# Rotary casts on ScalarE, quarter steps on VectorE and a new slot table in a two-layer pipeline

## The reference

```python
# block 1, per row: 16 heads of 16
xn = rms(x) * g1;  Q, K, V = xn @ Wq.T, xn @ Wk.T, xn @ Wv.T;  Q, K = elu(Q), elu(K)
kv1 = sum_h K[:, h, :8]^T V[:, h] * s     # two 8x16 matrices per row
kv2 = sum_h K[:, h, 8:]^T V[:, h] * s
attn = Q1 kv1 - lmb * Q2 kv2              # per head, then rms per head * g2, rms per row * g3 + itself
out = gelu(attn @ W1.T) @ W2.T + attn
# block 2: 16 segments of 512 rows
q, k, v = rms(h) @ Wq, @ Wk, @ Wv         # 16 query heads, 4 key heads, rotary embedding on q and k
ctx = causal_softmax(q k^T / 4) v;  h = clip(h + ctx @ Wo)
w = top 2 of 8 of softmax(rms(h) @ Wr);  out = clip(h + sum_e w_e * (silu(h Wg_e) * (h Wu_e)) Wd_e)
```

## Time and profile before

| what | value |
|---|---|
| median of 3 runs | 4241.21 us |
| the profiled execution | 4237.51 us, span 4235.6 us |
| PE, DVE, ACT, POOL busy | 3146.7, 2483.6, 1599.7, 1651.6 us |
| granted PE clock, mean | 0.843 of 2.4 GHz |
| attention_kernel | to about 3250 us |
| experts_kernel and finish | from about 3250 us to the end |

### The profile page before, as it was taken

The page is one execution under the profiler, slowest core; times in us unless marked ns, Lnnn a source line. Parts: engine busy times, 40 slices in busy tenths (PEclk is TensorE's granted clock), DMA queues, the critical chain, the costliest instruction groups (busy, mean ns, idle before and its releaser), DMA issues. The chain is left out here.

```text
span 4235.6 us, 54665 instructions
## 1 busy us (share of the span) xinstructions
PE 3146.7 (74%) x17668; PEld 1857.1 (44%) x17669; DVE 2483.6 (59%) x5036; ACT 1599.7 (38%) x3644; POOL 1651.6 (39%) x2045
## 2 busy tenths in 40 slices
PE   3555777777767776777777677767887399999991
PEld 2433434443443444444434444443433266666660
DVE  4667776776677667767776776676563122222225
ACT  1222445444534443443345444435544122222223
POOL 4564433543553354345435443541312122222222
PEclk7677888788888888887888888888888699999995
DMA  1000000000000000000000000000000533333335
GB/s 36 3 9 7 7 9 9 10 19 7 22 14 14 14 15 21 9 19 9 20 7 20 16 13 13 14 17 6 21 16 30 161 61 55 55 60 56 55 52 164
DMA packets 102336, 123.25 MB, mean 29 GB/s; under 512 B 14048, under 2 KB 89824, under 8 KB 102112
## 3 DMA queue, kind: packets, MB, share of 16 engines
q1 hardware_dynamic: 76384, 85.54, 6.7%
q0 software_dynamic: 25728, 34.88, 4.8%
HBM read 58.23 MB, written 61.36 MB: 28 GB/s over the span
## 5 line engine op out<-in xcount | busy, mean ns | idle before, releaser
L752 ACT ACTIVATE PR<-SP_ 128x512 f32<-128x512 f32 (+3 forms) x1536 | 728.0, 490 | 1528.6 <-PE SP_ L1366 1019.0
L1042 DVE TENSOR_REDUCE NM<-MX 128x1 f32<-128x512 f32 (+3 forms) x1536 | 817.1, 551 | 657.3 <-PE MX L1322 398.2
L1319 PE MATMUL MX<-KST,QST 96*128 96x512 bf16 (+3 forms) x1536 | 540.6, 362 | 407.3 <-DVE NM L1042 353.9
L472 POOL TENSOR_TENSOR P<-QK,VS 128x2048 f32<-128x2048 f32 x128 | 478.8, 3740 | 860.8 <-DVE QK L863 860.8
L1363 PE MATMUL SP_<-QST,KST 99*128 99x512 bf16 (+3 forms) x1536 | 544.0, 357 | 67.4 <-ACT PR L752 53.7
L1319 PEld LDWEIGHTS MX<-KST,QST 96*128 96x128 bf16 x1536 | 155.8, 102 | 770.5 <-DVE NM L1042 560.4
L1646 POOL DMA_INDIRECT scratch_h<-Y,XG x136 | 211.6, 1556 | 632.4 <-DVE Y L1709 538.8
L1214 PE MATMUL SUM<-ident,P 128*128 128x128 f32 x2048 | 313.0, 319 | 138.1 <-POOL P L472 83.5
L1687 DVE TENSOR_TENSOR AG<-UB,SL 128x512 f32<-128x512 f32 x136 | 94.0, 691 | 488.5 <-PE UB L1726 488.5
L1380 PE MATMUL OA<-PR,V 128*32 128x512 f32 (+3 forms) x3072 | 354.4, 536 | 0.8 <-ACT PR L752 0.6
L1214 PEld LDWEIGHTS SUM<-ident,P 128*128 128x128 f32 x2048 | 285.3, 168 | 158.3 <-issue 68.8
(11 more groups left out here) (245 smaller groups left out, 5399.1 us busy)
## 6 DMA issues: line engine op xcount, KB each, us to landing
XG<-scratch_xs SPq DMA_DIRECT2D x136, 130.0 KB, 2.1
X<-in_L_attn_x SPq DMA_DIRECT2D x64, 128.0 KB
scratch_x<-X SPq DMA_DIRECT2D x64, 128.0 KB, 1.8
scratch_h<-H SPq DMA_DIRECT2D x64, 128.0 KB, 1.7
X<-scratch_x SPq DMA_DIRECT2D x16, 512.0 KB, 4.0
HH<-scratch_h SPq DMA_DIRECT2D x16, 512.0 KB
out<-X SPq DMA_DIRECT2D x16, 512.0 KB, 3.2
wg<-in_L_ffn_Wg SPq DMA_DIRECT2D x1, 4096.0 KB, 13.9
```

The costliest lines, as they stand in the source:

```text
L472: sg["prod1"].by(pool.tensor_tensor(P1[:, half].rearrange("p (h e d) -> p h e d", h=hh, e=HD), QK[:, t % 2, D:2 * D][:, r].rearrange("p (h ...
L752: sg["exp"].by(act.activation(PR[:, n % 8, q0:512], SP_[:, n % 2, q0:512], ACT.Exp))
L1042: sg["mx"].by(dve.tensor_reduce(NM[:, u % 2, part, i, h:h + 1], MX[:, index % 2, 0:n], AX.X, ALU.max, negate=True))
L1319: m = pe.matmul(out, QST[0:MROW, j % 2, g * G + h, i * P:(i + 1) * P], KST[0:MROW, keys % RK, g, 0:n], start=True, stop=not last)
```

## The change

1. **Casts to ACT.** DVE's `parts` is taken apart. DVE keeps the add and two subtractions (`add_rotated`, `first_rest`, `third_part`); the two casts and the copy become ACT steps `first_part`, `second_part`, `second_again`. Each hand-over is a semaphore wait. They stand in slots DVE 7, ACT 8, DVE 9, ACT 10, DVE 11 and ACT 11; POOL's `copies` goes from slot 4 to 12.
2. **Quarter steps.** P2 has two buffers of half the size; the products and sums come in eight instructions of 128x1024 (slots 16 to 23, 0 and 1).
3. **Logits ahead.** PE's `second_layer` goes to slot 3, ahead of `route` (slot 5); DVE's `logits` stands in slot 7. Logits are thus copied a full period before the next second layer.
4. **New slots.** Most other steps move by a few slots.

```diff
-        P2 = sb("P2", [P, H * D // 2])
+        P2 = sb("P2", [P, 2, H * D // 4])
@@ POOL
-                        if i == 2 and have(p):
+                        if i == 4 and have(p):
                             key_products(p, 0)
-                        if i == 4 and have(p - 8):
-                            copies(p - 8)
-                        if i == 6 and have(p):
+                        if i == 7 and have(p):
                             key_products(p, 1)
-                        if i == 8 and have(p - 1):
+                        if i == 9 and have(p - 1):
                             head_roots(p - 1)
                         if i == 10 and have(p - 6):
                             out_coefficients(p - 6)
+                        if i == 12 and have(p - 8):
+                            copies(p - 8)
@@ ACT
+                def first_part(t):
+                    need("turned", t + 1)
+                    if t >= 1:
+                        need("tpq", 2 * t)
+                        need("copies", 3 * t)
+                    sg["part1a"].by(act.activation(parts_of_all(0), whole, ACT.Copy))
+
+                def second_part(t):
+                    need("rest", t + 1)
+                    sg["part1b"].by(act.activation(parts_of_all(1), rest, ACT.Copy))
+
+                def second_again(t):
+                    need("part1b", t + 1)
+                    sg["part2q"].by(act.activation(q_stack[:, :, 5], q_stack[:, :, 1], ACT.Copy))
...
+                        if i == 8 and have(p - 8):
+                            first_part(p - 8)
+                        if i == 10 and have(p - 8):
+                            second_part(p - 8)
+                        if i == 11 and have(p - 8):
+                            second_again(p - 8)
+                        if i == 11 and have(p - 6):
+                            layer_normed(p - 6)
                         if i == 12 and have(p - 7):
                             projected(p - 7)
-                        if i == 13 and have(p - 6):
-                            layer_normed(p - 6)
+                        if i == 14 and have(p):
+                            sums_out(p)
@@ DVE
-                def query_products(t, half):
+                def query_products(t, k):
                     need("kv", t + 1)
-                    need("attn", 2 * t + half)
+                    need("attn", 4 * t + k - 1)
...
-                    elif k == 1:
-                        sub.settle(dve)
-                        sg["part1"].by(dve.tensor_tensor(rest, whole, parts_of_all(0), ALU.subtract))
-                        need("part1", 2 * t + 1)
-                        sg["part1"].by(dve.tensor_copy(parts_of_all(1), rest))
...
+                def first_rest(t):
+                    need("part1a", t + 1)
+                    need("turned", t + 1)
+                    sg["rest"].by(dve.tensor_tensor(rest, whole, parts_of_all(0), ALU.subtract))
...
-                            query_sums(p - 1, 1)
-                        if i == 1 and have(p - 8):
-                            parts(p - 8, 0)
-                        if i == 2 and have(p):
-                            elu(p)
+                            query_products(p - 1, 3)
+                        if i == 1 and have(p - 1):
+                            query_sums(p - 1, 3)
+                        if i == 3 and have(p + 1):
+                            x_statistics(p + 1)
+                        if i == 4 and have(p):
+                            elu(p)
+                        if i == 5 and have(p - 6):
+                            add_attention(p - 6)
+                        if i == 6 and have(p - 1):
+                            head_squares(p - 1)
+                        if i == 7 and have(p - 18):
+                            logits(p - 18)
+                        if i == 7 and have(p - 8):
+                            add_rotated(p - 8)
+                        if i == 9 and (p - 22) % CH == 0 and have(p - 22):
                             place((p - 22) // CH)
+                        if i == 9 and have(p - 8):
+                            first_rest(p - 8)
                         if i == 11 and have(p - 17):
                             add_context(p - 17)
+                        if i == 11 and have(p - 8):
+                            third_part(p - 8)
...
+                        if i == 16 and have(p):
+                            query_products(p, 0)
+                        if i == 17 and have(p):
+                            query_sums(p, 0)
@@ PE
-                        if i == 4 and have(p - 18):
+                        if i == 3 and have(p - 6):
+                            second_layer(p - 6)
+                        if i == 5 and have(p - 18):
                             route(p - 18)
-                        if i == 5 and have(p - 6):
-                            second_layer(p - 6)
-                        if i == 8 and have(p):
+                        if i == 11 and have(p):
                             sum_heads(p, 0)
+                        if i == 13 and have(p):
+                            sum_heads(p, 1)
                         if i == 13 and have(p - 8):
                             stack_keys(p - 8)
-                        if i in (14, 15) and have(p - 8):
-                            stack_queries(p - 8, i - 14)
-                        if i == 16 and have(p):
-                            sum_heads(p, 1)
+                        if i == 15 and have(p):
+                            turn_sums(p)
+                        if i == 15 and have(p - 8):
+                            stack_queries(p - 8, 0)
...
-                        if i == 20 and have(p):
-                            turn_sums(p)
```

## The result

The changed kernel takes 3967.06 us (median of 4 runs, 3946.68 to 3974.67); the kernel before takes 4240.99 beside it. The ratio is 0.9347, 95% interval 0.9317 to 0.9378, so 274 us or 6.5% faster. On a second chip the same kernel came to 0.9313 (0.9298 to 0.9329). The forecast was 3961 us. The profiled execution took 3946.68 us, 290.8 us less than that of before.

The account below looks back on a forecast made before the run. No engine is full; waits between engines bound the kernel, chiefly PE's behind one blocked DVE cast. Light -120, heavy -146 and the rest -14 give -280 us on 4237.5, 3957.5, plus 3.7 for the median: 3961 us, range 3840 to 4125.

Parts of the forecast that it names:

- The block: DVE's second cast, 0.33 us at its shortest, lasts 3.67 beside POOL's first key product, so logits come late and PE idles.
- the second cause of the gap: PE's second layer waits for DVE to copy the previous tile's logits, 181.3 us in all; copying a period earlier removes it.
- the term for the gap itself: PE's waiting plus slow clock removed: 6.3 + 1.3 = 7.6 us a light period, 6.9 + 1.3 = 8.2 a heavy one.
- light periods: Four shorter periods in each cycle of eight, 42.9 us each before; mean gain 5.2 us, 23 x 5.2 = 120 us.
- The second term: Light period, end of `turn_sums` to end of next `elu`: 11.6 us before, 15.3 forecast.
- the sign of being right: Light periods of 34 to 37 us, key transposes waiting for POOL's `copies`; heavy periods of 47 to 49 us.
- the first term of the period: Light period, end of `elu` (q) to end of `turn_sums`, set by POOL's chain then ACT: 28.0 us before, 18.1 forecast.
- heavy periods: Four longer periods in each cycle of eight, 54.4 us each before; gain 6.1 us, 24 x 6.1 = 146 us.
- Finer DVE steps: Heavy periods: quarter steps let PE run on better at the period's end; counted at nothing, bound 1.5 us.
- what is late next: Delays replacing the gap: POOL's chain, then ACT, in light periods; eight steps, hand-overs and `first_rest` (0.6, 0.5, 1.0 us) in heavy.
- Rival B: Block moves to other DVE instructions beside POOL's products; 3.0 us of PE a period, 141 us back, about 4102 us; chance 0.20.
- Rival C: Chain of DVE-ACT hand-overs delays PE, 1.5 us each, 7.0 us a period, 329 us: slower, about 4290 us; chance 0.08.

Follow-up runs that it names:

- Early parts alone: Kernel before with all of DVE's rotary parts issued in slot 1, ahead of `elu`, casts still on DVE: ratio 0.9653, 147 us faster.
- the first expectation: Expected 4077 us for the kernel before with only `second_layer` ahead of `route` and DVE's `logits` behind `add_attention`; measured ratio 0.9928, about 30 us.
- the products late: Changed kernel with `turn_sums` back in PE slot 20 and DVE's eight product and sum steps in slots 20 to 1: ratio 0.9529.
- half steps: Changed kernel with products and sums back in four instructions of 128x2048 through one buffer: ratio 0.9375.
- casts back: Changed kernel with the two casts and the copy back on DVE, in their neighbours' slots 7, 9, 11: ratio 0.9369.
- the two small edits: Kernel before with DVE's rotary parts ahead of `elu` and PE's second layer ahead of the router matmul, `logits` behind the addition: ratio 0.9623.
- taking the rotary meetings away: Changed kernel with the rotary chain on DVE and ACT moved to slots where POOL runs no product: ratio 0.9323.
- one swap: Changed kernel with POOL's `out_coefficients` (slot 9) put ahead of `head_roots` (slot 10): 3882.11 us, ratio 0.9136.

## Why the prediction was right, and where not

**The block: right cause, priced too high.** The second cast met POOL's product in 56 of 64 tiles, DVE's queue stood, and PE waited for whatever came next in it. Early parts alone gave 147 us. The prediction named the order of the logits as the second cause of the gap, and the first expectation gave it 164 us; alone it brought 30, as its wait went to the addition behind the same cast, and with the block gone 13 or nothing. The larger error is in the term for the gap itself. The forecast took 7.6 us of each light period and 8.2 of each heavy one, 372 us in the 47. Taking away the meeting and the order gave 157.6: 41.1 us a light period for 42.8, and 49.1 a heavy one for 54.1. That run also puts 1.5 us of DVE's steps ahead of `elu`, so the bare gap may be worth up to 1.5 us a period more (an estimate from the durations of those four steps), but not 7.6 or 8.2. The idle time before the second layer was read as if a period would get shorter by all of it; when it went, other waits of PE grew: at the router matmul for the addition (74.8 us), before the head sums for POOL's products (115.0 against 83.5) and before `stack_queries` for ACT's `k_stacked` (46.6 against 16.5).

**The light periods, right in mechanism, too hopeful in size.** The forecast cut the period at the end of `elu` and the end of `turn_sums`: 18.1 + 15.3 us. In the period shown it is 1420.57 to 1441.17 = 20.6, then to 1456.78 = 15.6. The second term was right within 0.3 us. The first was 2.5 us short. ACT's part of it was nearly right: `layer_normed` starts at q + 14.5 (14.0 forecast) and `sums_out` ends at q + 18.1 (17.5). But the sum went from there straight to `turn_sums`, and PE was not free. The key transposes were taken to wait for POOL's copies (q + 14.7), but they wait for the bank behind ACT's `projected` (they start at q + 16.2). So PE works off them and the units behind them, on the lower clock after the idle time, until 1440.00, and `turn_sums` takes 1.17 us and not 0.61. The router's wait of 1.65 us, for an addition that it now stands close to, was not in the sum; in this period it lies ahead of the longer wait for the keys, so what it costs is not shown. Light periods gained 3.8 us on the mean (42.8 to 39.0) and not 5.2, and came to 39.0 where the sign of being right was 34 to 37. The longer two of the four, which the forecast put nearer the full 7.6, gained 5.5 and 2.9. This is the step that failed on the light side: the first term of the period, 20.6 and not 18.1.

**The heavy periods, too low.** 7.1 us gained (54.1 to 46.9), 6.1 forecast. The step that failed is "Finer DVE steps should let PE run on better at the end of the period; I count that at nothing", and with it that the earlier start of the products had no gain of its own: undoing the earlier start makes a heavy period 1.4 us longer, undoing the finer steps 0.9 (46.9 to 48.4 and 47.8). Both make a light period longer too, by 1.0 each, so they also hide part of the light periods' error.

**The sum: a good deal of luck.** 266 us were forecast for the 47 periods, 258.8 came. By period type that is an error of 32 us in the light ones (120 and 87.8) against one of -25 in the heavy ones (146 and 171.0). By cause the cancelling is larger. The forecast was 372 us for the gap less 106 for what is late next; the runs show 157.6 with the block and the order away, and 101 more by everything else in the change, which the forecast had as a loss. Three parts of that rest, each undone by itself, cost 84 us (the products late), 19 (half steps) and 17 (casts back), 120 together over the whole kernel, against the some 120 that the two small edits left open; so no large part of the change is unaccounted for, though such parts need not add up. The mechanism that the forecast named is the largest single one and was shown by itself, but it is some 60% of the gain in the stretch and not all of it. The first sixteen periods gave 24 us (14 forecast), the tail 8 (0).

**Rival B.** Instructions on DVE with both inputs in SBUF do block for as long as a product lasts: `first_rest` took 1.06 to 3.88 us in the 16 of 64 tiles in which it met one. The Trainium skill says that such an instruction contends with a GpSimd one that reads SBUF ("SBUF — State Buffer", section "Who interferes with whom"); the trace agrees. But the rival's price was 3.0 us of PE a period beyond the 1.0 counted for heavy ones, and taking the rotary meetings away brought nothing measurable in all. The reason that the forecast gave, POOL's chain being longer anyway, fits the light periods, which gained nothing; the heavy ones gained 0.6 us each (1126.5 to 1111.1), near the 1.0 that the forecast had counted there.

**Rival C.** The hand-overs make ACT wait for DVE, 67.5 us in all before the first cast and 81.9 before the second, 2.3 us a tile, and over 1 us for each, which the prediction had called a sign of this rival if PE waits for exponentials with it. PE does so for 72.6 us (53.7 before), but still for 67.5 with the casts back on DVE, where there are no hand-overs. So these waits lie mostly beside others, and putting the casts back made nothing faster.

## What to carry to other kernels

Find the instruction whose duration has two values (0.33 and 3.67 us here) before asking who waits: the waits behind it change their name when steps are reordered (30 us gained here), while its own removal shortens them (147 us). But don't count the idle time behind it as gained: 8 us a period were counted and 3.4 came, as other waits came up. When a step moves up in one queue, look at what it itself waits for on the slowest queue; the cheapest edit of this study, worth nearly a third of the change once more, was one swap on an engine that was 42% busy. And spread long steps over the stretch in which others need short answers: starting them sooner and spreading them was worth 84 us, and the prediction had given it no gain.

## What the runs showed of the hardware beside that

A tensor-tensor instruction of 128x320 takes 0.48 us alone and up to 3.88 beside a POOL product of 3.67; reductions, and additions with one input in PSUM, keep their time there (L938: 0.41 us in 57 of 64 cases beside a product). A clip between two constants, one input of 128x256 float32 (L977, TENSOR_SCALAR), takes 0.29 us alone and 1.18 to 2.31 in the 10 of 64 cases beside a product. POOL's power instruction on 128x16 takes 2.92 us.

Runs of the changed kernel spread over 28 us on one chip (3946.68 to 3974.67) and 17 on another, those of the kernel before over 4 to 13 on five occasions, of the one with the rotary steps moved over 36, of the swapped one over 4.3. So the meetings of the rotary steps are not needed for a wide spread; what causes it stays open.
